# Three edits to the Mamba layer of a four-layer kernel: taps of two conv blocks in turn, tokens that arrive turned, three small products as transposes

## The chip, the cores and the metric

The kernel runs on one core of one Trainium2 chip. Time is device microseconds (us) of one execution. The kernel before took 1125.33, 1127.39 and 1128.77 us in three runs (median 1127.39). The engines are named as in the profile: PE (TensorE, matmuls), PEld (its weight loads), DVE (VectorE), ACT (ScalarE), POOL (GpSimd), SP (SyncE, which here only issues DMAs). Each runs its own instructions in program order, and waits on semaphores for the others.

## The reference

Four layers, each followed by a residual sum and a layer norm, on 2048 tokens of 512 features in float32. All of the change lies in the first, a Mamba-2 mixer over two sequences of 1024 tokens:

```python
zxbcdt = einsum('bld,di->bli', x, W_in)          # gate 1024, xBC 1024+16+16, dt 16
conv = conv_b
for k in range(4):
    conv = conv + xpad[:, k:k + l, :] * conv_w[:, k]
xBC = silu(conv)                                  # -> x (16 heads of 64), B, C
dt = softplus(dt + dt_bias);  dA = exp(dt * -exp(A_log))
h = h * dA + (dt * x) B ;  y = h C                # scan over the tokens
y = (y + D_skip * x) * silu(gate)
y = y * rsqrt(mean(y * y) + eps) * norm_w
x = layernorm(x + einsum('bld,do->blo', y, W_out))
```

The three layers behind it (a ternary product bounded by tanh, an RG-LRU block, a gated FFN on int32 codes) are the same in both kernels.

## The kernel before, in words

Features lie on the 128 partitions, tokens along the free dimension. Every float32 product is made of three fp32r products: each operand is split into a high part (`..h`, a rounded copy made by ACT) and a low part (`..l`, the difference, made by DVE), and `three` in the PE's program multiplies high by high, high by low and low by high.

`mamba2` works in 8 steps s = 0 to 7, alternately of the one sequence and of the other. A step is 256 tokens, two chunks j of 128. No scheduler orders anything: each engine has a function (`sync`, `gpsimd`, `scalar`, `vector`, `tensor`) with a loop over s that is written out by hand, and work of step s+1 is started in the second half of step s. The parts that the prediction speaks of are these.

- Turning the tokens. SP loads the tokens of a step into `a_xf`, tokens on partitions. `turn` on PE (line 809) transposes them in 8 blocks into the banks `ps_t`, `turn` on ACT (393) copies them rounded into `a_xth`, `turn` on DVE (583) makes `a_xtl`. PE does it for s+1 right behind the last gate product of step s, DVE between `cumulate(s)` and the second `scan`.
- Projections. `x_proj` (8 blocks m, in pairs p) and `gate` (the same) are 96 matmuls of 256 columns each per step; `out_proj` 24 of 512 columns per chunk. All have line 801, that of `three`.
- The convolution. ACT's `evict` (443, 446) copies a pair of blocks to `a_xpre` and writes the fourth tap with the bias into `a_xs`. On DVE `conv_m` adds the other three taps to one block by `taps` (575): each tap reads and writes the same tile as the tap before it, and `order` makes DVE wait for its end. There are 8 blocks a step, so 24 taps and 16 such waits. Between them stand `low` (701) and the pieces of the norm: `mean_sq` (615), `residual` (623, 625, 627), `normalize` (633). `residual` needs `a_rs`, which POOL's `scale` (338) makes from what `mean_sq` wrote.
- The decays. ACT's `decay` and `bc_out` (414 to 419) give the decays and C; `turn_a` (829) before them and `gram` (836, 838) behind them are small PE products; `turn_z` (822) is another. ACT's `gram` (424, 426) copies the result to `a_btok` and `a_gs`, and the PE's `out_proj` of the second chunk may start only when `a_gs` has been read out of its bank.
- The scans. DVE's `scan` (658) runs four scans of 512 elements per chunk over `a_L`, `cumulate` (646) four of 128 over `a_ex`, each with a wait for the one before it though they write different parts.
- The end of a step. DVE updates the state (680), adds the outputs from the banks (688), gates them (695), and makes the decays of the next step (`soft`, 596 to 610). ACT's `high_y` (434) and `square` (438) need the gated values, and `decay` comes behind them in ACT's order. POOL's `tree` (331 to 333) sums the squares.

Of the kernel before, what the change touches and what calls it, by code (L numbers as in the profile page):

```python
# [59 lines left out]
class Order:  # L60
# [5 lines left out]
    def __call__(self, ins):  # L66
        self.count += 1
        ins.then_inc(self.sem, 1)
        self.eng.wait_ge(self.sem, self.count)
# [14 lines left out]
def mamba2(nc, signals, psum, ident, powers, x_in, x_out, da_d, c_d, w_x, w_bc, w_gate, w_out, conv, a_log, dt_bias, d_skip, norm_w, fill, space, following):  # L84
# [35 lines left out]
    xf = sb("a_xf", [P, C, D], F32)  # L120
# [55 lines left out]
    s_xt, s_xh, s_xl = sem("xt"), sem("xh"), sem("xl")  # L176
# [43 lines left out]

    def sync(sp, following_stage):
        def load_x(s):
            for j in range(C):
                wait(sp, s_xt, C * (s - 1) + j + 1)
                sp.dma_start(xf[:, j, :], chunk(x_in, s, j)).then_inc(s_x[j], 16)
# [44 lines left out]
        for s in range(NS):  # L270
# [8 lines left out]
            else:  # L279
                if s == NS - 1:  # L280
                    sp.wait_ge(s_xt, C * NS)
# [96 lines left out]
    def scalar(act, following_stage):  # L378
# [180 lines left out]
    def vector(dve, following_stage):  # L559
        order = Order(dve, s_dve)  # L560

# [73 lines left out]
        def conv_m(s, m):  # L635
            i = M * s + m
            dve.wait_ge(s_acc, i + 1)
            dve.wait_ge(s_pre, 4 * s + m // 2 + 1)
# [13 lines left out]
        def scan(n):  # L652
# [142 lines left out]
    def tensor(pe, following_stage):  # L795
# [1247 lines left out]
```

## Time and profile before

| | before |
|---|---|
| three runs, us | 1125.33, 1127.39, 1128.77 |
| span of the profiled execution, us | 1127.5 |
| PE, PEld busy, us | 1076.4, 939.6 |
| DVE, ACT, POOL busy, us | 749.1, 572.9, 318.6 |
| granted TensorE clock, mean | 0.980 |
| the Mamba layer, us from the start | 0 to about 445 |

The profiled execution is given by its span, from the first to the last instruction; it is 0.1 us from the median of the runs. "Busy" is the time in which at least one instruction of an engine was running; for PE the ends are modelled, and its share of busy time overstates how full it is. DVE is 96% busy in the steps of the Mamba layer and 31% in the last layer, so shares are read by stage.

### The profile page before, as it was taken

Reading aid. Unit: us, or ns where it says so; the run is one execution under the profiler, and the core shown is the slowest. Engines: PE = TensorE matmul, PEld = TensorE weight load, DVE = VectorE, ACT = ScalarE, POOL = GpSimd, SP = SyncE. Lnnn points to the kernel's source line nnn. Section 1 sums busy time; section 2 is a strip of 40 time slices with the busy share of each in tenths; the row PEclk is TensorE's granted clock in tenths of the full one; section 3 lists DMA queues with packets and bytes.
Section 4 is the critical chain, followed back from the end, with each engine's and each line's share of the span. In section 5 each row is a group of like instructions: output and inputs, shape, how many; then the busy total and the mean of one; then the engine's idle time right before and its main releaser. Section 6 shows DMA issues by size and latency. Waiting matters only on the chain.

```text
span 1127.5 us, 18155 instructions
## 1 busy us (share of the span) xinstructions
PE 1076.4 (95%) x6912; PEld 939.6 (83%) x6912; DVE 749.1 (66%) x1311; ACT 572.9 (51%) x1190; POOL 318.6 (28%) x433
## 2 busy tenths in 40 slices
PE   6899999999999997899999999899999999999997
PEld 6788888888888886788998998887888888888886
DVE  6899999999999988857766687765342233223213
ACT  6857666667757674565666556653312311321320
POOL 1012222130403123333444434414312311321331
PEclk9889999999999998999999999999999999999999
DMA  5504031312213055411011101408012002002001
GB/s 198 200 3 147 12 137 45 103 52 95 91 57 126 3 201 198 143 55 38 1 38 39 39 1 39 141 19 299 0 38 75 1 19 94 1 1 75 1 1 56
DMA packets 41590, 81.22 MB, mean 72 GB/s; under 512 B 7456, under 2 KB 13472, under 8 KB 39456
## 3 DMA queue, kind: packets, MB, share of 16 engines
q1 hardware_dynamic: 41504, 80.06, 21.2%
q8 instruction: 55, 0.90, 0.3%
q14 instruction: 31, 0.25, 0.1%
HBM read 67.19 MB, written 12.85 MB: 71 GB/s over the span
## 4 chain that ended last, share of the span: by engine, by line
PE 57%; DVE 26%; ACT 7%; issue 6%; POOL 3%; DMA 2%; DVEq 0%; SPq 0%; POOLq 0%; ACTq 0%
PE banks L1870 20%; PE banks L1883 11%; PE banks L801 9%; PE banks L1518 8%; DVE a_L L658 5%; DVE a_xs L575 4%; PE banks L1486 4%; PE banks L931 2%; DVE a_ygl L701 1%; DVE a_L L672 1%; DVE c_gx L1377 1%; PE banks L923 1%; DMA c_xb<-tokens 1%; ACT c_a L1252 1%; DVE a_stats L625 1%
## 5 line engine op out<-in xcount | busy, mean ns | idle before, releaser
L1770 ACT ACTIVATE d_sg<-banks,d_gs 128x512 f32<-128x512 f32 x64 | 44.0, 688 | 224.9 <-PE banks L1870 224.9
L1813 DVE SCALAR_TENSOR_TENSOR d_h<-banks,d_us,d_sg 128x512 f32<-128x512 f32 x64 | 48.1, 751 | 163.7 <-PE banks L1870 151.3
L1744 POOL TENSOR_TENSOR d_hl<-d_h,d_hh 128x512 fp32r<-128x512 f32 x64 | 83.2, 1300 | 158.3 <-ACT d_hh L1774 158.2
L575 DVE SCALAR_TENSOR_TENSOR a_xs<-a_xpre,a_cvec,a_xs 128x256 f32<-128x256 f32 x192 | 100.3, 537 | 7.1 <-ACT a_xs L446 2.5
L1883 PE MATMUL banks<-d_wd,d_hh 128*128 128x512 f32 x256 | 101.1, 395 | 0.0
L1883 PE MATMUL banks<-d_wd,d_hl 128*128 128x512 f32 x256 | 100.9, 394 | 0.0
L331 POOL TENSOR_TENSOR a_sg<-a_sg 128x512 f32<-128x512 f32 x16 | 24.6, 1535 | 220.1 <-ACT a_sg L438 220.1
L658 DVE TENSOR_TENSOR_SCAN a_L<-a_L,a_ident 128x512 f32<-128x512 f32 x64 | 78.4, 1225 | 2.2
L801 PE MATMUL banks<-a_xth,a_wxh 128*128 128x256 f32 x256 | 76.7, 299 | 0.0
L462 ACT ACTIVATE a_xdt<-banks,a_dt 128x64 f32<-128x64 f32 x256 | 56.3, 349 | 37.1 <-PE banks L881 37.1
L801 PE MATMUL banks<-a_xth,a_wgh 128*128 128x256 f32 x256 | 75.0, 293 | 0.0
L801 PE MATMUL banks<-a_xtl,a_wxh 128*128 128x256 f32 x256 | 74.1, 289 | 0.0
L801 PE MATMUL banks<-a_xth,a_wxl 128*128 128x256 f32 x256 | 74.0, 289 | 0.0
L801 PE MATMUL banks<-a_xth,a_wgl 128*128 128x256 f32 x256 | 72.9, 285 | 0.0
L801 PE MATMUL banks<-a_xtl,a_wgh 128*128 128x256 f32 x256 | 72.8, 284 | 0.0
L801 PE MATMUL banks<-a_woh,a_ygh 128*128 128x512 f32 x128 | 55.0, 429 | 5.6 <-ACT a_gs L426 3.7
L1883 PEld LDWEIGHTS banks<-d_wd,d_hl 128*128 128x128 f32 x256 | 48.1, 188 | 11.2
L1883 PEld LDWEIGHTS banks<-d_wd,d_hh 128*128 128x128 f32 x256 | 48.2, 188 | 11.0
L801 PEld LDWEIGHTS banks<-a_xth,a_wxh 128*128 128x128 f32 x256 | 50.5, 197 | 4.7 <-issue 4.1
L801 PE MATMUL banks<-a_woh,a_ygl 128*128 128x512 f32 x128 | 52.7, 412 | 0.0
L801 PE MATMUL banks<-a_wol,a_ygh 128*128 128x512 f32 x128 | 52.6, 411 | 0.0
L1870 PE MATMUL banks<-d_xtl,d_wg_late 128*128 128x512 f32 x128 | 51.5, 402 | 0.0
(285 smaller groups left out, 3151.9 us busy)
## 6 DMA issues: line engine op xcount, KB each, us to landing
a_L<-decays SPq DMA_DIRECT2D x16, 1024.0 KB, 5.2
a_xf<-in_x SPq DMA_DIRECT2D x16, 256.0 KB, 3.1
a_xr<-in_x SPq DMA_DIRECT2D x16, 256.0 KB, 2.8
tokens<-a_xr SPq DMA_DIRECT2D x16, 256.0 KB, 4.0
c_xb<-tokens SPq DMA_DIRECT2D x16, 256.0 KB, 3.2
d_xin<-tokens SPq DMA_DIRECT2D x16, 256.0 KB, 4.8
d_r<-tokens SPq DMA_DIRECT2D x16, 256.0 KB, 2.7
d_wd_codes<-in_down_w SPq DMA_DIRECT2D x4, 1024.0 KB, 9.4
```

Source lines behind the costliest of these rows:

```text
L331: order(pool.tensor_tensor(sq[:, 0:4], sq[:, 0:4], sq[:, 4:8], ALU.add))
L462: ins = act.activation(xdt[:, j, h * HD:(h + 1) * HD], ps_t[:, q % 2, 2 * j + i // 2, i % 2 * HD:(i % 2 + 1) * HD], ACT.Copy, scale=dt[:, ...
L575: ins = dve.scalar_tensor_tensor(out=dst, in0=src[:, k:k + T], scalar=vec[:, k:k + 1], in1=dst, op0=ALU.mult, op1=ALU.add)
L658: order(dve.tensor_tensor_scan(own, own, ident4.rearrange("p h t -> p (h t)"), 0.0, ALU.mult, ALU.add))
L801: last = pe.matmul(out, lhs(i, k), rhs(c, k), start=(k, i, c) == (0, 0, 0), stop=(k, i) == (n - 1, 1))
L1486: done = pe.matmul(ps_x, x[:, k, cols(j)], wp[:, k, :], start=i == 0, stop=i == 3 * KD - 1)
L1518: done = pe.matmul(ps_x[:, q, m % 2, :], wp[:, k, m * P:(m + 1) * P], x[:, k, :], start=i == 0, stop=i == 3 * KD - 1)
L1744: pool.tensor_tensor(hl[:, m, :], h32[:, m % 2, :], hh[:, m, :].bitcast(F32), ALU.subtract).then_inc(s_hl, 1)
L1770: act.activation(sg[:, m % 2, :], ps_g[:, m % 2, :], ACT.Silu, scale=gs[:, m:m + 1]).then_inc(s_sg, 1)
L1813: dve.scalar_tensor_tensor(out=h32[:, m % 2, :], in0=ps_u[:, m % 2, :], scalar=us[:, m:m + 1], in1=sg[:, m % 2, :], op0=ALU.mult, op1=ALU. ...
L1870: ins = pe.matmul(out[:, m % 2, :], w(k, m), x[:, k, :], start=(k == 0 and x is xth), stop=(k == KD - 1 and x is xtl))
L1883: ins = pe.matmul(ps_o[:, c % 2, :], h[:, m, cols(c)], wd[:, m, :], start=(m == 0 and h is hh), stop=(m == M - 1 and h is hl))
```

## The change

On DVE the taps of two blocks alternate: tap 0 of block 2p, tap 0 of block 2p+1, tap 1 of block 2p, and so on, where each tap from the second on waits for the tap before it on its own block. `Order` gets two halves for that: `mark` counts an instruction, `after` waits for a count. The scans of `scan` and `cumulate` are marked and no longer waited for one by one; the first instruction that reads their result waits for the last. `low` and the two `mean_sq` move to the places between pairs.

The host hands the tokens over a second time, turned (`x_turned`), features on partitions. `a_xf` has the same size and is loaded from there; ACT and DVE make `a_xth` and `a_xtl` from it, and PE's `turn` is gone with its waits. ACT's `turn` now waits until the gate products that read `a_xth` are done, SP's next load waits for DVE's `turn` and no longer for PE's.

Three small PE products with the identity (`turn_z`, `turn_a`, the first half of `gram`) are written as transposes.

```diff
     def __call__(self, ins):
+        self.after(self.mark(ins))
+
+    def mark(self, ins):
         self.count += 1
         ins.then_inc(self.sem, 1)
-        self.eng.wait_ge(self.sem, self.count)
+        return self.count
+
+    def after(self, count):
+        self.eng.wait_ge(self.sem, count)
...
             for j in range(C):
-                wait(sp, s_xt, C * (s - 1) + j + 1)
-                sp.dma_start(xf[:, j, :], chunk(x_in, s, j)).then_inc(s_x[j], 16)
+                wait(sp, s_xl, C * (s - 1) + j + 1)
+                sp.dma_start(xf[:, ks(j), :], x_turned[s % B * NT + s // B, :, ks(j), :]).then_inc(s_x[j], 16)
...
         def turn(s):
+            wait(act, s_gate, 4 * s)
             for j in range(C):
-                act.wait_ge(s_xt, C * s + j + 1)
-                act.activation(xth[:, :, cols(j)], ps_t[:, j], ACT.Copy).then_inc(s_xh, 1)
+                act.wait_ge(s_x[j], 16 * s + 16)
+                act.activation(xth[:, ks(j), :], xf[:, ks(j), :], ACT.Copy).then_inc(s_xh, 1)
...
-                dve.tensor_tensor(xtl[:, :, cols(j)], ps_t[:, j], xth[:, :, cols(j)].bitcast(F32), ALU.subtract).then_inc(s_xl, 1)
+                dve.tensor_tensor(xtl[:, ks(j), :], xf[:, ks(j), :], xth[:, ks(j), :].bitcast(F32), ALU.subtract).then_inc(s_xl, 1)
...
+        def conv_pair(s, p):
+            pair = (2 * p, 2 * p + 1)
+            tapped = {}
+            dve.wait_ge(s_pre, 4 * s + p + 1)
             wait(dve, s_halo, s)
-            taps(xs[s % 2][:, m, :], xpre[:, m, :], cvec[:, m, :], s_xc)
+            for k in range(3):
+                for m in pair:
+                    out = xs[s % 2][:, m, :]
+                    if k == 0:
+                        dve.wait_ge(s_acc, M * s + m + 1)
+                    else:
+                        order.after(tapped[m])
+                    ins = dve.scalar_tensor_tensor(out=out, in0=xpre[:, m, k:k + T], scalar=cvec[:, m, k:k + 1], in1=out,
+                                                   op0=ALU.mult, op1=ALU.add)
+                    if k < 2:
+                        tapped[m] = order.mark(ins)
+                    else:
+                        ins.then_inc(s_xc, 1)
...
                 for j in range(C):
-                    order(dve.tensor_tensor_scan(ex[:, g, cols(j)], ex[:, g, cols(j)], zero.broadcast_to([P, P]), 1.0, ALU.mult, ALU.add))
+                    last = order.mark(dve.tensor_tensor_scan(ex[:, g, cols(j)], ex[:, g, cols(j)], zero.broadcast_to([P, P]), 1.0, ALU.mult, ALU.add))
             wait(dve, s_su, G * C * s)
+            order.after(last)
...
-                order(dve.tensor_tensor_scan(own, own, ident4.rearrange("p h t -> p (h t)"), 0.0, ALU.mult, ALU.add))
+                scanned[j] = order.mark(dve.tensor_tensor_scan(own, own, ident4.rearrange("p h t -> p (h t)"), 0.0, ALU.mult, ALU.add))
...
             wait(dve, s_stp, n - C + 1)
+            order.after(scanned[j])
...
-            conv_m(s, 4)
+            conv_pair(s, 2)
             if s:
                 mean_sq(C * s - 2)
-            conv_m(s, 5)
-            if s:
                 mean_sq(C * s - 1)
                 residual(C * s - 2)
-            conv_m(s, 6)
-            conv_m(s, 7)
+            conv_pair(s, 3)
...
-        def turn(s):
-            for j in range(C):
-                pe.wait_ge(s_x[j], 16 * s + 16)
-                wait(pe, s_xdt, 4 * (s - 1) + 2 + j + 1)
-                for k in range(KD):
-                    last = pe.transpose(ps_t[:, j, k, :], xf[:, j, k * P:(k + 1) * P], ident)
-                last.then_inc(s_xt, 1)
...
-                last = pe.matmul(ps_f[0:H, cols(j)], a[:, j, :], ident, start=True, stop=True)
+                last = pe.transpose(ps_f[0:H, cols(j)], a[:, j, :], ident)
...
             pe.wait_ge(s_xs, 4 * s + q + 1)
-            if q < 2:
-                pe.wait_ge(s_xl, C * s + q + 1)
-            else:
-                pe.wait_ge(s_xdt, 4 * s + q - 2 + 1)
+            wait(pe, s_xdt, 4 * s + q - 2 + 1)
...
     dram("x", x.reshape(-1, P, D))
+    dram("x_turned", x.reshape(-1, 2 * P, KD, P).transpose(0, 3, 2, 1))
```

On DVE, from the last gating of a step to the first `residual` of the next; in brackets stands what a row waits for (`a_dve_order` is DVE's own earlier work). Before:

```order
L695 TENSOR_TENSOR a_xs_81<-a_xs_81,a_sg 128x8x128 [waits a_sg,a_ya]
L575 SCALAR_TENSOR_TENSOR a_xs_99<-a_xpre,a_cvec,a_xs_99 128x256 [waits a_halo,a_pre,a_acc]
L575 SCALAR_TENSOR_TENSOR a_xs_99<-a_xpre,a_cvec,a_xs_99 128x256 [waits a_dve_order] x2
L701 TENSOR_TENSOR a_ygl_93<-a_xs_81,a_ygh_91 128x1024 [waits a_yh]
...
L615 TENSOR_SCALAR a_rs<-banks 128x1 [waits a_ssqp]
L575 SCALAR_TENSOR_TENSOR a_xs_99<-a_xpre,a_cvec,a_xs_99 128x256 [waits a_halo,a_pre,a_acc]
L575 SCALAR_TENSOR_TENSOR a_xs_99<-a_xpre,a_cvec,a_xs_99 128x256 [waits a_dve_order] x2
L615 TENSOR_SCALAR a_rs<-banks 128x1 [waits a_ssqp]
L623 SCALAR_TENSOR_TENSOR a_xr<-banks,a_rs,a_xr 128x512 [waits a_rs,a_xr0,a_op]
```

And now, in the changed kernel's line numbers (658 the taps, 726 `low`, 626 `mean_sq`, 634 `residual`):

```order
L720 TENSOR_TENSOR a_xs_81<-a_xs_81,a_sg 128x8x128 [waits a_sg,a_ya]
L658 SCALAR_TENSOR_TENSOR a_xs_99<-a_xpre,a_cvec,a_xs_99 128x256 [waits a_acc,a_halo,a_pre]
L658 SCALAR_TENSOR_TENSOR a_xs_99<-a_xpre,a_cvec,a_xs_99 128x256 [waits a_acc]
L658 SCALAR_TENSOR_TENSOR a_xs_99<-a_xpre,a_cvec,a_xs_99 128x256 [waits a_dve_order] x4
L726 TENSOR_TENSOR a_ygl_93<-a_xs_81,a_ygh_91 128x1024 [waits a_yh]
...
L626 TENSOR_SCALAR a_rs<-banks 128x1 [waits a_ssqp] x2
L634 SCALAR_TENSOR_TENSOR a_xr<-banks,a_rs,a_xr 128x512 [waits a_rs,a_xr0,a_op]
```

`low` has moved behind three more taps, the first `mean_sq` has gone back behind the taps of block 5, and the three taps that stood between it and `residual` no longer do.

On PE, from the end of `gate(s, 3)` to the next step's first product (909, now 918, is `state`; 923 and 931, now 932 and 940, are `scan_out`). Before:

```order
L801 MATMUL banks<-a_xth,a_wgl 128x256
L809 MATMUL banks<-ident,a_xf 128x128 x8
L909 MATMUL banks<-a_xdt,a_bw 64x256 x4
L923 MATMUL banks<-a_ex,a_S 128x128 x8
L931 MATMUL banks<-a_L_82,a_xdt 64x128 x16
```

And now:

```order
L821 MATMUL banks<-a_xth,a_wgl 128x256
L918 MATMUL banks<-a_xdt,a_bw 64x256 x4
L932 MATMUL banks<-a_ex,a_S 128x128 x8
L940 MATMUL banks<-a_L_82,a_xdt 64x128 x16
```

The 8 transposes of the tokens are gone; nothing else has changed places on PE.

## Rows read from the trace of the kernel before

**Rows 1.** The page: the span, and the busy time of each engine.
```profile
span 1127.5 us, 18155 instructions
PE 1076.4 (95%) x6912; PEld 939.6 (83%) x6912; DVE 749.1 (66%) x1311; ACT 572.9 (51%) x1190; POOL 318.6 (28%) x433
```

**Rows 2.** Busy time by stretch; columns as in the first line.
```profile
core 0: us, PE busy (x) PEld busy (x) DVE busy (x) ACT busy (x) POOL busy (x), PEclk, DMA share, GB/s
186.57:237.93 51.36, 49.84 (x409) 44.38 (x408) 49.22 (x87) 35.32 (x88) 12.12 (x17) 1.00 0.25 81
```

**Rows 3.** Waits of DVE in 83.7 to 340 us: total, times, longest.
```profile
DVE a_xs L688 <- PE banks L931: 0.9, 5, 0.2
```

**Rows 4.** DVE in order of time: start, us, line, tiles, times; around step 3.
```profile
183.91 1.52 DVE L575 SCALAR_TENSOR_TENSOR a_xs<-a_xpre,a_cvec,a_xs 128x256 f32<-128x256 f32 x3
193.71 0.15 DVE L615 TENSOR_SCALAR a_rs<-banks 128x1 f32<-128x1 f32 x1
212.94 1.28 DVE L583 TENSOR_TENSOR a_xtl<-banks,a_xth 128x512 fp32r<-128x512 f32 x2
214.30 5.00 DVE L658 TENSOR_TENSOR_SCAN a_L<-a_L,a_ident 128x512 f32<-128x512 f32 x4
223.88 0.87 DVE L680 SCALAR_TENSOR_TENSOR a_S<-a_S,a_et,a_tmp 128x256 f32<-128x256 f32 x2
235.27 1.53 DVE L575 SCALAR_TENSOR_TENSOR a_xs<-a_xpre,a_cvec,a_xs 128x256 f32<-128x256 f32 x3
```

**Rows 5.** ACT in order of time, step 3.
```profile
189.49 0.42 ACT L419 ACTIVATE a_cs<-a_bcs 16x256 f32<-16x256 f32 x1
211.01 0.60 ACT L475 ACTIVATE a_sg<-banks 128x512 f32<-128x512 f32 x1 [0.94 <-PE banks L801]
211.51 1.08 ACT L393 ACTIVATE a_xth<-banks 128x512 fp32r<-128x512 f32 x2
```

**Rows 6.** PE in order of time, step 3.
```profile
191.04 0.60 PE L860 MATMUL banks<-a_ones,a_sg 128*128 128x1 f32 x4
192.06 0.47 PE L801 MATMUL banks<-a_woh,a_ygh 128*128 128x512 f32 x1 [0.41 <-ACT a_gs L426]
210.69 0.28 PE L801 MATMUL banks<-a_xth,a_wgl 128*128 128x256 f32 x1
210.81 1.03 PE L809 MATMUL banks<-ident,a_xf 128*128 128x128 f32 x8
235.03 0.61 PE L829 MATMUL banks<-ident,a_a 128*16 128x128 f32 x4
```

**Rows 7.** POOL in order of time, step 3.
```profile
193.94 0.72 POOL L338 TENSOR_TENSOR a_rs<-a_rs,powers 128x1 f32<-128x1 f32 x1 [4.75 <-DVE a_rs L615]
```

**Rows 8.** Groups: line, tiles, shapes, times, busy us, mean ns.
```profile
L658 DVE TENSOR_TENSOR_SCAN a_L<-a_L,a_ident 128x512 f32<-128x512 f32 x64 | 78.4, 1225 | 2.2
L1377 DVE TENSOR_TENSOR_SCAN c_gx<-c_a,c_hlast,c_gx 128x256 f32<-128x256 f32 x32 | 21.4, 733 | 0.3
L452 ACT ACTIVATE a_xs<-a_xs 128x512 f32<-128x512 f32 x32 | 20.4, 665 | 0.0
L393 ACT ACTIVATE a_xth<-banks 128x512 fp32r<-128x512 f32 x16 | 8.6, 596 | 0.0
```

**Rows 9.** DVE in order of time, the RG-LRU layer and step 6.
```profile
506.39 2.68 DVE L1377 TENSOR_TENSOR_SCAN c_gx<-c_a,c_hlast,c_gx 128x256 f32<-128x256 f32 x4
338.14 1.52 DVE L575 SCALAR_TENSOR_TENSOR a_xs<-a_xpre,a_cvec,a_xs 128x256 f32<-128x256 f32 x3
367.92 1.29 DVE L583 TENSOR_TENSOR a_xtl<-banks,a_xth 128x512 fp32r<-128x512 f32 x2 [0.65 <-ACT a_xth L393]
```

**Rows 10.** Busy time behind the small products of steps 5 and 6.
```profile
294.90:298.30 3.40, 3.37 (x17) 2.84 (x18) 3.26 (x10) 0.93 (x2) 0.86 (x2) 1.00 0.80 309
347.60:351.00 3.40, 3.40 (x11) 2.62 (x10) 3.28 (x8) 0.00 (x0) 1.27 (x2) 0.50 0.42 138
```

**Rows 11.** The chain that ended last, at `turn_z(1)`: start, us, what.
```profile
61.49 1.03 PE banks L822 x4
```

More of the change, by code:

```diff
@@ L81, in inverse_root, with mamba2 @@
     return pool.tensor_tensor(out, v, powers[:, 1:2].broadcast_to(v.shape), ALU.pow)
-def mamba2(nc, signals, psum, ident, powers, x_in, x_out, da_d, c_d, w_x, w_bc, w_gate, w_out, conv, a_log, dt_bias, d_skip, norm_w, fill, space, following):
+def mamba2(nc, signals, psum, ident, powers, x_in, x_turned, x_out, da_d, c_d, w_x, w_bc, w_gate, w_out, conv, a_log, dt_bias, d_skip, norm_w, fill, space, following):
     T = 256
@@ L119, in mamba2 @@
     at_xf = sb.at
-    xf = sb("a_xf", [P, C, D], F32)
+    xf = sb("a_xf", [P, KD, T], F32)
     xpre = sb("a_xpre", [P, M, HALO + T], F32)
@@ L175, in mamba2 @@
     s_x, s_xr, s_st = ([sem(f"{n}{j}") for j in range(C)] for n in ("x", "xr", "st"))
-    s_xt, s_xh, s_xl = sem("xt"), sem("xh"), sem("xl")
+    s_xh, s_xl = sem("xh"), sem("xl")
     s_bp, s_bcr, s_bacc, s_bconv, s_bhalo, s_cs = (sem(n) for n in ("bp", "bcr", "bacc", "bconv", "bhalo", "cs"))
@@ L219, in rows, with ks @@
         return slice(r * 64, (r + 1) * 64)
+    def ks(j):
+        return slice(j * KD // C, (j + 1) * KD // C)
     def sync(sp, following_stage):
@@ L280, in sync @@
                 if s == NS - 1:
-                    sp.wait_ge(s_xt, C * NS)
+                    sp.wait_ge(s_xl, C * NS)
                     following_stage["load_x"](0)
@@ L560, in vector @@
         order = Order(dve, s_dve)
+        scanned = {}
         def low_piece(i):
@@ L633, in normalize @@
             dve.tensor_scalar(out, out, mv[:, j, 0:1], mv[:, j, 2:3], ALU.subtract, ALU.mult).then_inc(s_done, 1)
[L635 to L638, printed above, removed]
+        def conv_pair(s, p):
+            pair = (2 * p, 2 * p + 1)
+            tapped = {}
+            dve.wait_ge(s_pre, 4 * s + p + 1)
             wait(dve, s_halo, s)
-            taps(xs[s % 2][:, m, :], xpre[:, m, :], cvec[:, m, :], s_xc)
+            for k in range(3):
[11 more added lines that the diff above has]
+                        ins.then_inc(s_xc, 1)
         def cumulate(s):
@@ L716, in vector @@
         for s in range(NS):
-            conv_m(s, 0)
+            conv_pair(s, 0)
             if s:
                 low(C * s - 1)
-            conv_m(s, 1)
-            if s == 0:
+            else:
                 low_piece(NX)
                 low_piece(NX + 1)
-            conv_m(s, 2)
-            conv_m(s, 3)
+            conv_pair(s, 1)
             if s == 0:
@@ L821, in turn_z @@
             for j in range(C):
-                last = pe.matmul(ps_f[:, 256 + j * H:256 + (j + 1) * H], bcr[Z0:Z0 + H, HALO + j * P:HALO + (j + 1) * P],
-                                 ident[Z0:Z0 + H, Z0:Z0 + H], start=True, stop=True)
+                last = pe.transpose(ps_f[:, 256 + j * H:256 + (j + 1) * H], bcr[Z0:Z0 + H, HALO + j * P:HALO + (j + 1) * P],
+                                    ident[Z0:Z0 + H, Z0:Z0 + H])
             last.then_inc(s_zt, 1)
@@ L835, in gram @@
             for j in range(C):
-                pe.matmul(ps_f[:, j * N:(j + 1) * N], bcs[0:N, cols(j)], ident[0:N, 0:N], start=True, stop=True)
+                pe.transpose(ps_f[:, j * N:(j + 1) * N], bcs[0:N, cols(j)], ident[0:N, 0:N])
             for j in range(C):
@@ L933, in scan_out @@
                 last.then_inc(s_yp, 1)
-        pe.wait_ge(s_const, 2)
-        turn(0)
         pe.wait_ge(s_const, 15 + HQ)
@@ L966, in tensor @@
             gate(s, 3)
-            if s + 1 < NS:
-                turn(s + 1)
-            else:
+            if s + 1 == NS:
                 following_stage["turn_in"](0)
@@ L1938, in build @@
             split.append((raw, d[name].rearrange("(k p) n -> p k n", p=P), *W[n]))
-        first, last, parts, ends = mamba2(nc, signals, psum, ident, powers, x, between[0], decays, readouts, d["w_x"], d["w_bc"], d["w_gate"],
+        first, last, parts, ends = mamba2(nc, signals, psum, ident, powers, x, d["x_turned"], between[0], decays, readouts, d["w_x"], d["w_bc"], d["w_gate"],
                                           d["w_out0"], d["conv0"], d["A_log"], d["dt_bias"], d["D_skip"], d["norm_w"], fill_identity,
```

## The prediction

> **What bounds the kernel now.** I read the busy shares first. PE is busy 95% of the span and DVE 66% [rows 1], which would leave DVE out of it. By stage it looks otherwise: in a whole step of the Mamba layer DVE is busy 49.22 of 51.36 us, and PE 49.84, whose ends are modelled [rows 2]. So the waits come next. Over the five steps from 83.7 to 340 us DVE waits for another engine for 0.9 us in all, always at the same place, the last outputs from the banks [rows 3]. DVE thus sets the pace of these steps: each of its instructions starts when the one before it allows.
>
> I call E the start of the first tap of a step. E is 183.91 us in step 3 and 235.27 in step 4 [rows 4], so a step takes 51.36 us. DVE being full does not say what a faster DVE is worth. For that I follow the other way round the loop, from E through ACT and PE back to DVE. Gating ends at E; then ACT runs `high_y`, `square`, the decays and C without a gap, and `a_cs` is done at 189.91 (E + 6.0) [rows 5]. PE makes its small products, waits for ACT's copy `a_gs`, and starts `out_proj` of the second chunk at 192.06 (E + 8.15) [rows 6]. From there PE has no wait until the last gate matmul of 210.69 ends at 210.97. ACT's silu starts at 211.01, `a_xth` at 211.51 [rows 5, 6], and DVE's `turn` comes at 212.94, E + 29.03 [rows 4]. The two `a_xth` take 596 ns each [rows 8], so the first is there at 211.51 + 0.60 = 212.11. DVE comes only 0.8 us later than it could. That slack of 0.8 us in the first half of a step, against a DVE gain larger than it, is the heart of this forecast.
>
> **The change part by part, per full step.**
>
> Taps. Three taps on one block take 1.52 us from the start of the first to the end of the last [rows 4]; two pairs of start to start of 0.52 and one run of 0.48. Where two instructions of 256 elements don't depend on each other, `a_S`, both together take 0.87 us at 0.48 each [rows 4], so the second starts 0.39 after the first. The cost of a dependence is thus 0.52 - 0.40 = 0.12 us, and 16 of the 24 taps have one: 1.92 us. Alternating, a tap is called 0.8 us after the tap that it needs, which ends after 0.48. I take 0.12; the ends are 0 and 0.13 each, from the same rows.
>
> Scans. Four scans in a row take 5.00 us, the last of them 1.225 [rows 4, 8], so they start (5.00 - 1.225) / 3 = 1.26 apart: 0.035 goes to each wait. A scan without a wait stands in the RG-LRU layer: four take 2.68 us at 0.733 each [rows 8, 9], 0.65 apart, against the 0.77 that 0.733 and 0.035 would give. Saving 0.12 each: 4 x 0.12 = 0.48 per chunk, once in each half of the step. The four small scans of `cumulate` give 3 x 0.12 = 0.36, in the first half. Bounds 0 and 0.15 each.
>
> Residual. The two `mean_sq` now stand together right ahead of `residual`, which needs POOL's power of the first. POOL starts 0.23 us after `mean_sq` and takes 0.72 [rows 4, 7] (193.71, 193.94 to 194.66). Before, three taps lay over it; now DVE waits from 0.14 to about 1.00 us: +0.86. Behind `residual` in DVE's queue stand the last six taps, the scans and `turn`. Bounds 0.5 and 1.2, the power's 0.72 us taken half as long and half as long again.
>
> DVE reaches `turn` at 29.03 - 1.92 - 0.48 - 0.36 + 0.86 = E + 27.13. It can't start before `a_xth`, at 212.11 + 0.04 = 212.15, E + 28.24. ACT and PE take what they took on that way, since none of their work on it is touched but two small products: `gram` loses two instructions of 0.11 us, yet `a_gs` follows ACT's own queue, which stands before it. So `turn` comes at 28.24 instead of 29.03: 0.8 us earlier, not 1.9. The new residual wait is hidden in the 1.1 us that DVE would wait anyway. POOL's `tree` lies beside the first taps as before.
>
> `a_xth` and `a_xtl` now read the SBUF instead of a bank. ACT takes 665 ns for 512 elements from there in `a_xs` and 596 from a bank [rows 8]: between -0.05 and +0.07 us; I take 0.
>
> From `turn` to the next E is 235.27 - 212.94 = 22.33 us [rows 4]. Of it goes 0.48 by the scans of the second chunk. PE has lost its 8 transposes, 1.03 us [rows 6], just ahead of `state`; it comes 1.0 us earlier there, and so keeps ahead of a DVE that is 0.8 earlier. `turn_a` and `turn_z` lose two instructions each, 0.61 us for four [rows 6], so 0.2 to 0.3 us; neither ends a wait of DVE. They cost nothing and give nothing here. The second half becomes 21.85.
>
> A step: 28.24 + 21.85 = 50.09, down 1.27 us. Steps 1 to 5: -6.4.
>
> SP. The next load of `a_xf` waits for DVE's `turn`, some 2 us later than for PE's. Behind it in SP's queue is the transfer of the decays, 25 us away. Nothing.
>
> Step 0 and the start. The first `x_proj` waits for the weights, not for the tokens. `turn_z(1)` lies on the chain that ended last, at half clock, 1.03 us for four [rows 11]: -0.4.
>
> Steps 6 and 7. Here `turn` waited for `a_xth` already: it comes at 367.92, 29.78 behind E at 338.14, with 0.65 us of waiting [rows 9]. Only the second half gains: -0.5 each, -1.0.
>
> **The clock.** In step 6, behind the small products and the wait for `a_gs`, PE ran at 0.50 of its clock, 1.2 instead of 2.4 GHz, from 347.6 to 351.0; at the same place of step 5 at 1.00 [rows 10]. Step 7 has the same fall. It cost PE 29.78 - 28.24 = 1.5 us, of which DVE's slack took half. Now no slack is left, and each such fall costs the whole 1.5. And they may come more often: PE reaches the small products 0.2 us earlier and has two fewer of them, so it idles longer in front of `a_gs`, where it idled 0.41 us in step 3 [rows 6]. How many of steps 1 to 5 fall I can't read; the trace has none of five there and two of two in steps 6 and 7. I take two: +3.0. The ends are none and all five (+7.5).
>
> In the Trainium skill, "TensorE: Matmul & The Clock Gate", Part 4: PE-mode transpose, says that work in transpose mode does not count as PE being busy in the same way. Here 8 transposes of the tokens ran in 1.03 us with the clock at 1.00 in that whole step [rows 2, 6]; whether the three small ones matter no row tells. By the rule more steps would fall, up to the end of all five, 1127.2 by the sum below.
>
> **Sum.** 1127.5 (the span, 0.1 from the median) - 6.4 - 0.4 - 1.0 + 3.0 = 1122.7. I say 1122.5. What comes after 445 us is unchanged and starts earlier by the same amount.
>
> **Rivals.**
>
> The clock falls in every step: 1127.5 - 7.8 + 7.5 = 1127.2. For it: no slack, more idling. Against: five of seven steps were free of it.
>
> The clock falls no more than before: 1119.7.
>
> DVE gets all that it saves, because ACT and PE come earlier too: 51.36 - 1.92 - 0.96 - 0.36 + 0.86 = 48.98 a step, 2.4 less, times seven 16.7: 1110.8. Against it stand the 18.9 us of PE work without a gap from `a_gs` to the last gate matmul [rows 6], which nothing shortens.
>
> Slower: the waits cost nothing, so taking them away gives nothing, while the residual wait stands. Then `turn` is at 29.03 + 0.86 and the second half at 22.33: 0.86 more a step, times seven 6.0, less 0.4: 1133.1. It decides once taps and scans of the first half save less than 0.86 of the 2.76 us counted. That is what the Trainium skill would give: "VectorE: DVE Perf Modes", The DRAIN you can't avoid, says that the next operation starts only when the pipeline is empty, that eight copies took the same with a semaphore after each as with one at the end, and that semaphores need not be saved. Against it: the pair `a_S` overlaps by 0.09 us and the four scans by 0.08 each [rows 4, 9], at full length in each row. This row is of this kernel, and I follow it.
>
> **Numbers.** One to three more falls of the clock, 1121 to 1124.5: 0.43. None more: 0.25. Four or five: 0.17. All of DVE's gain: 0.06. Slower by the residual wait: 0.09. No change means within 0.3%, 3.4 us, of 1127.4, about what can be told apart here: 1124.0 to 1130.8. Faster then holds 0.25, 0.06 and most of the first, 0.35: 0.66. The same: the rest of the first, 0.16 of the clock in every step and 0.02 of the last: 0.26. Slower: 0.08. The range leaves out the fourth case and most of the last: 1114 to 1129.
>
> **What would show it.** In the changed profile: taps of a pair in 2.4 us (0.40 apart) instead of 2.9; four scans in 4.6 to 4.7; a wait of DVE for POOL ahead of `residual` of 0.8 to 0.9 us; a new wait of DVE's `turn` for ACT's `a_xth` near 1.1 us; E + 28.2 for `turn`; steps of 50.1 us at full clock and of 51.6 with a fall. I am wrong if `turn` doesn't wait (then DVE's own sum decides), if taps stand 0.52 apart, or if full-clock steps are not 1.0 to 1.5 us shorter.

## The result, and the profile after

| | before | after |
|---|---|---|
| median, us (15 executions each) | 1128.5 (1125.33 to 1130.57) | 1123.06 (1121.81 to 1126.62) |
| ratio, 95% interval | | 0.9961 (0.9952 to 0.997) |
| span of the profiled execution, us | 1127.5 | 1123.2 |
| mean granted clock in it | 0.980 | 0.975 |

The changed kernel is 0.39% faster: 5.4 us between the medians, where 4.9 against the first median of 1127.4 had been forecast. The page shows where instructions went: PE has 112 fewer, DVE as many as before but 15.8 us less busy [rows 1].

```profile
span 1123.2 us, 17876 instructions
PE 1061.2 (94%) x6800; PEld 927.2 (83%) x6800; DVE 733.3 (65%) x1311; ACT 573.0 (51%) x1190; POOL 321.8 (29%) x433
```

The steps come next. By stretch, the changed kernel: step 1 (whole at full clock), step 3 (with a fall of the clock), then the falls of steps 2 to 5 and 7, and the same place of step 6, which has none (columns as in [rows 2]).

```profile
80.98:130.85 49.87, 47.92 (x396) 42.93 (x396) 47.01 (x88) 35.14 (x87) 12.85 (x16) 1.00 0.26 84
182.62:233.94 51.32, 49.40 (x396) 44.02 (x395) 47.10 (x87) 35.13 (x87) 12.85 (x16) 0.97 0.25 81
139.31:142.72 3.41, 3.41 (x10) 2.63 (x9) 2.68 (x9) 0.46 (x1) 1.07 (x2) 0.50 0.72 271
190.51:193.92 3.41, 3.28 (x8) 2.63 (x9) 2.71 (x9) 1.02 (x2) 1.06 (x2) 0.50 0.80 305
241.71:245.12 3.41, 3.15 (x8) 2.51 (x9) 2.71 (x9) 1.15 (x3) 0.97 (x2) 0.50 0.78 305
292.91:296.32 3.41, 2.88 (x7) 2.33 (x8) 2.72 (x10) 1.42 (x5) 0.70 (x2) 0.50 0.87 321
395.31:398.72 3.41, 3.41 (x10) 2.66 (x9) 2.68 (x7) 0.01 (x1) 1.07 (x2) 0.50 0.62 210
344.10:347.50 3.40, 2.88 (x13) 2.35 (x14) 2.70 (x10) 1.42 (x5) 0.69 (x2) 1.00 0.90 323
```

The steps without a fall take 49.87 us (step 1) and 49.80 (step 6), against 51.36 of [rows 2]. Those with one take 51.2 to 51.8. So five falls stand at this place in steps 1 to 7 where the trace before had two. (Falls from 33 us behind the last E on, where the layer ends, stand in every kernel's trace and are not counted.) From E of step 1 to E of step 7 it is 305.4 us, after 309.3: 3.9 less, where six steps of 49.85 would give 10.2 less.

DVE's side of step 1 (start, duration, both us; a wait and its releaser in brackets):

```profile
80.98 2.46 DVE L658 SCALAR_TENSOR_TENSOR a_xs<-a_xpre,a_cvec,a_xs 128x256 f32<-128x256 f32 x6
91.88 0.75 DVE L634 SCALAR_TENSOR_TENSOR a_xr<-banks,a_rs,a_xr 128x512 f32<-128x512 f32 x1 [0.70 <-POOL a_rs L347]
109.10 1.30 DVE L594 TENSOR_TENSOR a_xtl<-a_xf,a_xth 128x512 fp32r<-128x512 f32 x2 [0.90 <-ACT a_xth L403]
110.46 4.57 DVE L682 TENSOR_TENSOR_SCAN a_L<-a_L,a_ident 128x512 f32<-128x512 f32 x4
```

Six taps take 2.46 us, where two blocks took 2.9 [rows 4]; four scans 4.57 where they took 5.00. `turn` comes at E + 28.12, after 0.90 us of waiting for `a_xth`. DVE's waits in 80 to 340 us (total, times, longest) answer to [rows 3], which had one row:

```profile
DVE a_xtl L594 <- ACT a_xth L403: 8.7, 5, 2.0
DVE a_xr L634 <- POOL a_rs L347: 3.5, 5, 0.7
DVE a_xr L634 <- PE banks L821: 1.2, 4, 0.4
DVE a_xs L713 <- PE banks L940: 0.9, 5, 0.2
```

DVE now waits 14.3 us in five steps. The first row is the cap of the first half: 0.9 in the step at full clock and 2.0 in the four with a fall. PE and ACT at the small products of step 1:

```profile
86.36 0.28 PE L821 MATMUL banks<-a_xth,a_wxl 128*128 128x256 f32 x1
87.02 0.29 PE L848 MATMUL banks<-ident,a_bcs 16*128 16x16 f32 x2 [0.39 <-ACT a_cs L429]
87.17 0.69 PE L850 MATMUL banks<-a_cs,a_bcs 16*128 16x128 f32 x4
87.79 0.61 PE L872 MATMUL banks<-a_ones,a_sg 128*128 128x1 f32 x4
89.00 0.47 PE L821 MATMUL banks<-a_woh,a_ygh 128*128 128x512 f32 x1 [0.61 <-ACT a_gs L436]
```
```profile
86.88 0.57 ACT L453 ACTIVATE a_xpre<-banks 128x512 f32<-128x512 f32 x1
87.47 1.02 ACT L456 ACTIVATE a_xs<-banks,a_cvec 128x256 f32<-128x256 f32 x2
88.47 0.39 ACT L436 ACTIVATE a_gs<-banks 128x256 f32<-128x256 f32 x1
```

PE waits twice here, 0.39 for `a_cs` and 0.61 for `a_gs` (before: 0.41 for `a_gs` in the step of [rows 6], 0.56 to 0.57 in most others, and under 0.1 ahead of it), and starts `out_proj` of the second chunk at E + 8.02. ACT evicts the last pair of blocks (453, 456) between `a_cs` and `a_gs`: PE's products are there before ACT is free to copy them.

### The profile page after: what moved, and what is told of

Its sections match the earlier page's. It is cut to its first block, busy times and chain, and to the rows that moved or that the text cites. A ratio compares the mean times of both kernels' runs of the same rounds, so it can differ in the third digit from the quotient of the medians.

```text
span 1123.2 us, 17876 instructions
## 1 busy us (share of the span) xinstructions
PE 1061.2 (94%) x6800; PEld 927.2 (83%) x6800; DVE 733.3 (65%) x1311; ACT 573.0 (51%) x1190; POOL 321.8 (29%) x433
## 4 chain that ended last, share of the span: by engine, by line
PE 61%; DVE 18%; ACT 10%; issue 5%; POOL 3%; DMA 2%; SPq 1%; POOLq 0%; DVEq 0%; ACTq 0%
PE banks L1875 21%; PE banks L821 13%; PE banks L1888 11%; PE banks L1523 8%; PE banks L1491 4%; DVE a_L L682 2%; PE banks L940 2%; DVE c_gx L1382 1%; PE banks L890 1%; PE banks L932 1%; DVE a_ygl L726 1%; ACT L428 1%; ACT L424 1%; DVE c_cv L1358 1%; ACT a_xs L456 1%
## 5 line engine op out<-in xcount | busy, mean ns | idle before, releaser
L340 POOL TENSOR_TENSOR a_sg<-a_sg 128x512 f32<-128x512 f32 x16 | 31.1, 1943 | 223.7 <-ACT a_sg L448 223.7
L658 DVE SCALAR_TENSOR_TENSOR a_xs<-a_xpre,a_cvec,a_xs 128x256 f32<-128x256 f32 x192 | 90.1, 538 | 2.8 <-ACT a_xs L456 2.8
L682 DVE TENSOR_TENSOR_SCAN a_L<-a_L,a_ident 128x512 f32<-128x512 f32 x64 | 73.1, 1205 | 0.5
L821 PEld LDWEIGHTS banks<-a_xth,a_wxh 128*128 128x128 f32 x256 | 50.4, 197 | 5.1 <-issue 3.9
L1875 PE MATMUL banks<-d_xtl,d_wg_late 128*128 128x512 f32 x128 | 51.5, 402 | 0.0
```

What stands on the lines that cost most here:

```text
L340: order(pool.tensor_tensor(sq[:, 0:4], sq[:, 0:4], sq[:, 4:8], ALU.add))
L658: ins = dve.scalar_tensor_tensor(out=out, in0=xpre[:, m, k:k + T], scalar=cvec[:, m, k:k + 1], in1=out, op0=ALU.mult, op1=ALU.add)
L682: scanned[j] = order.mark(dve.tensor_tensor_scan(own, own, ident4.rearrange("p h t -> p (h t)"), 0.0, ALU.mult, ALU.add))
L821: last = pe.matmul(out, lhs(i, k), rhs(c, k), start=(k, i, c) == (0, 0, 0), stop=(k, i) == (n - 1, 1))
L1875: ins = pe.matmul(out[:, m % 2, :], w(k, m), x[:, k, :], start=(k == 0 and x is xth), stop=(k == KD - 1 and x is xtl))
```

## The experiments

Times are medians beside the kernel before on the same chip. The step is one at full clock in the profiled execution, E to E; "turn" is DVE's `turn` behind E, "rest" from there to the next E.

| kernel | us | ratio to before (95%) | step | turn | rest | mean clock of its timed executions |
|---|---|---|---|---|---|---|
| before | 1128.1 to 1129.4 | 1 | 51.36 | 29.03 | 22.33 | 0.983 (68) |
| changed | 1123.06 | 0.9961 (0.9952 to 0.997) | 49.87 | 28.12 | 21.75 | 0.978 (15) |
| scans_only | 1124.41 | 0.9955 (0.994 to 0.9969) | 50.78 | 28.32 | 22.46 | 0.984 (9) |
| taps_only | 1127.0 | 0.9977 (0.9964 to 0.999) | 50.83 | 28.37 | 22.46 | 0.983 (12) |
| turned_only | 1129.31 | 1.0005 (0.9991 to 1.002) | 51.37 | 29.04 | 22.33 | 0.982 (12) |
| small_undone | 1124.36 | 0.9972 (0.9959 to 0.9984) | 50.25 | 28.33 | 21.92 | 0.979 (11) |
| filler | 1117.27 | 0.9908 (0.9895 to 0.992) | 49.97 | 28.05 | 21.92 | 0.985 (4) |
| before_filler | 1127.02 | 0.9991 (0.998 to 1.0002) | 51.33 | 29.02 | 22.31 | 0.985 (11) |
| filler_mean | 1117.36 | 0.9905 (0.9889 to 0.9921) | 49.85 | 28.09 | 21.75 | 0.985 (5) |
| filler_turns | 1119.64 | 0.9919 (0.9903 to 0.9935) | 50.23 | 28.09 | 22.14 | 0.984 (6) |
| filler_serial | 1123.02 | 0.995 (0.9934 to 0.9965) | 50.99 | 29.07 | 21.92 | 0.983 (6) |
| gram_first | 1121.28 | 0.9942 (0.9928 to 0.9956) | 49.40 | 27.63 | 21.77 | 0.978 (6) |
| gram_filler | 1114.86 | 0.9883 (0.9868 to 0.9898) | 49.33 | 27.57 | 21.77 | 0.983 (4) |
| chain_short | 1111.81 | 0.986 (0.9845 to 0.9875) | 49.09 | 27.31 | 21.78 | 0.985 (4) |

### One part alone, put into the kernel before

scans_only is this, and the same in `cumulate`:

```diff
-                order(dve.tensor_tensor_scan(own, own, ident4.rearrange("p h t -> p (h t)"), 0.0, ALU.mult, ALU.add))
+                scanned[j] = order.mark(dve.tensor_tensor_scan(own, own, ident4.rearrange("p h t -> p (h t)"), 0.0, ALU.mult, ALU.add))
...
+            order.after(scanned[j])
```

> The kernel before with only the scans of scan and cumulate unmarked (one wait behind the last in place of one behind each). Theory 1, the loop from E over ACT and PE caps the first half at E + 28.1 to 28.2: DVE would reach turn at 29.03 - 0.48 - 0.36 = E + 28.19, which just meets that cap, and the second half becomes 22.33 - 0.48 = 21.85; steps at full clock of 50.0 to 50.1 us, steps with a fall of the clock of 51.4, so nearly all of the whole change's gain: 1123 to 1124.5 us, ratio 0.996. Rival, the parts add up in proportion to what they take off DVE (1.32 of 2.4 us net a step): 1125.5, ratio 0.9975. Rival, a wait between scans costs nothing: 1128.5.

taps_only takes `conv_pair` and the new places of `low` and `mean_sq`:

> The kernel before with only the taps in pairs and low and mean_sq in their new places; scans waited for one by one, tokens turned on PE. Theory 1: DVE would reach turn at 29.03 - 1.92 + 0.7 = E + 27.8, the cap makes it 28.2, the second half stays 22.3: 50.5 a step at full clock, 51.9 with a fall. With four falls in seven steps that is 2.3 us less than before: 1126, ratio 0.998; with none 5.6 less. Rival, the parts in proportion (1.06 of 2.4): 1126 as well, but then with steps of 50.1 at full clock and no wait of turn. Rival, slower by the wait for POOL: 1133.

turned_only takes `x_turned` and loses PE's `turn`:

> The kernel before with only the tokens handed over turned: 64 transposes less on PE, 1.03 us a step just ahead of state. Theory 1: PE's second half waits for nobody, and DVE for nobody in it: no difference, 1128 to 1129, ratio 0.9995 to 1.0005, steps of 51.4. Rival, PE bounds the second half: up to 1.0 a step, 1121.5.

Turned tokens alone give nothing, as both steps and the time say. taps_only has about the time that was expected, but steps of 50.8 and not 50.5: turn comes 0.2 us later and its second half is no shorter than before. The scans alone give as much time as the whole change, which rules out that parts count in proportion. The cap stood where it was put, turn at 28.3 to 28.4 in both kernels. But the second half of scans_only stayed at 22.46, although four scans in it are 0.43 shorter. Its waits of DVE, 83 to 340 us:

```profile
DVE a_xtl L590 <- ACT a_xth L399: 3.2, 2, 1.7
DVE a_z L595 <- PE banks L831: 2.6, 5, 0.5
```

The second row is new: 0.5 us in each step for `turn_z`. With PE's own transposes of the tokens left in, PE bounds the second half. So the steps are 50.8 and not 50.0; the time was still as forecast, because this execution had two falls in steps 1 to 7, and the clock over its timed executions is 0.984 against the changed kernel's 0.978. The whole change has steps 0.9 us shorter than scans_only and hands it back in falls.

### The clock

filler puts work that nobody reads into PE's two waits:

```diff
+        def filler(s, count):
+            wait(pe, s_xdt, 4 * s)
+            for k in range(count):
+                pe.matmul(ps_t[:, 0].rearrange("p k t -> p (k t)"), wo[0][:, k, 0:P], wo[0][:, k, :], start=True, stop=True)
...
             x_proj(s, 3)
+            if s:
+                filler(s, 2)
             gram(s)
...
             if s:
+                filler(s, 2)
                 out_proj(C * s - 1, 0)
```

> The changed kernel with four more PE products a step (512 columns, operands always there, result never read): two in the wait ahead of gram, two in the wait for a_gs. They compute nothing that is needed. Theory, the falls of the clock come from PE's idling at that place and cost up to 1.6 us each: no fall at that place in steps 1 to 7, steps of 49.9 to 50.0 us each, so six steps take 299.5 in place of 305.4 in the changed kernel's profile: 1117.5, ratio to before 0.990, mean granted clock 0.984 or more. Rival, the falls do not depend on how long PE idles there: as the changed kernel, 1123 to 1124, ratio 0.996. Rival, the added products are on the path (0.22 each): 1123 + 5 = 1128.

Measured: 1117.27 us, no fall in steps 1 to 7, all of them 49.8 to 50.4. PE at the place that follows step 4's E (231.52), and a whole step:

```profile
236.85 0.62 PE L871 MATMUL banks<-a_woh 128*128 128x512 f32 x2
237.56 0.30 PE L848 MATMUL banks<-ident,a_bcs 16*128 16x16 f32 x2
238.79 0.71 PE L871 MATMUL banks<-a_woh 128*128 128x512 f32 x2
239.54 0.47 PE L821 MATMUL banks<-a_woh,a_ygh 128*128 128x512 f32 x1
```
```profile
231.52:281.48 49.96, 48.92 (x400) 43.36 (x399) 47.17 (x87) 35.10 (x87) 12.78 (x16) 1.00 0.25 83
```

`out_proj` starts at E + 8.02, as without the filler: four more products cost nothing, and 5.8 us are gone. That products put into PE's idle time at this place take the falls away, and that every step then takes about 50, is shown. Then the same in the kernel before:

> The kernel before with the same four added products a step (they compute nothing that is needed), two ahead of gram and two ahead of out_proj of the second chunk. Theory: without falls in steps 1 to 7 all its steps take 51.4; a fall costs the kernel before only 0.9, DVE's slack taking the rest, and it has some two to four of them: 1126, ratio 0.998. Against filler's 1117.3 the change is then worth 9 us, where it was worth 5.4 with falls. Rival, a fall costs both kernels the same: the kernel before gains 6 as well, 1122.5, ratio 0.995.

Measured 1127.02, steps of 51.33 to 51.34: 1.3 us gained, inside the interval, near the theory and far from the rival's 6. Between the two fillers lie 9.75 us (1127.02 - 1117.27, on two chips whose kernels before differ by 0.1). That is what the change is worth when PE keeps its clock; 4.3 of it were lost to falls. There are more of them, and each costs 1.3 to 1.9 us where it cost 0.9 before (step 6, 52.23 against 51.36), DVE's slack hiding the rest.

small_undone has the three products as before:

> The changed kernel with the three small products as matmuls with the identity again. Theory: out_proj of the second chunk starts 0.28 later (E + 8.3, as in the runs of single parts), turn at 28.35 in place of 28.12, steps at full clock of 50.1; the idling is as long as in the changed kernel, so falls are as frequent: 1124 to 1125, ratio 0.9965. Rival, products in transpose mode do not count as work for the clock, so that as matmuls they prevent the falls: clock 0.984, 1118 to 1119, ratio 0.991.

Turn came at 28.2 to 28.4 in its three steps without a fall, and the clock is as low as the changed kernel's (0.979 and 0.978). Written as matmuls the products do not keep the clock. But one premise of the theory is not in the trace: PE does not idle here as long as in the changed kernel. Waits of PE in 83 to 340 us, the changed kernel first, then small_undone:

```profile
PE banks L821 <- ACT a_gs L436: 3.0, 5, 0.6
PE banks L848 <- ACT a_cs L429: 2.2, 5, 0.5
PE banks L821 <- ACT a_gs L436: 2.4, 5, 0.6
```

Added up from the timelines, gap by gap, PE's idle time between the last product of `x_proj` and `out_proj` of the second chunk is this, in steps 1 to 7, beside the mean clock of the timed executions:

| kernel | idle, us a step | mean clock |
|---|---|---|
| before, scans_only, taps_only, turned_only | 0.48 to 0.57 | 0.982 to 0.984 |
| small_undone | 0.47 to 0.57 | 0.979 |
| gram_first (below) | 0.5 to 0.7 | 0.978 |
| changed | 1.0 to 1.15 | 0.978 |
| filler, gram_filler (below) | 0 to 0.12 | 0.985, 0.983 |

Filling the idle time ends the falls. But its length does not tell how many there are: small_undone idles no longer than the kernel before and has the changed kernel's clock. Why the changed kernel falls more often stays open.

### The prediction's own steps, with the clock held

filler_mean, where `conv_pair` calls what it is given behind its first two taps:

```diff
-            conv_pair(s, 2)
+            conv_pair(s, 2, lambda: mean_sq(C * s - 2) if s else None)
             if s:
-                mean_sq(C * s - 2)
```

> filler with mean_sq of the first chunk put back between the taps of the third pair, so that residual need not wait for POOL (0.7 us a step). Theory, the wait is hidden behind turn's wait for a_xth, which becomes 1.5 in place of 0.9: steps of 50.0 as in filler, 1117.3, ratio 0.991. Rival, DVE sets the pace: 0.7 us less in each of seven steps, 1112.5, ratio 0.9865.

1117.36 against 1117.27. DVE's first wait, in 83 to 340 us, is now this, and the row on `a_rs` is gone; filler had 4.2 and 3.5:

```profile
DVE a_xtl L594 <- ACT a_xth L403: 8.3, 5, 1.7
```

The wait for POOL was moved into the wait for `a_xth`, nothing else. It was hidden, as forecast.

filler_turns has the tokens turned on PE:

> filler with the tokens turned on PE again (8 transposes a step ahead of state); taps, scans and small products as in the changed kernel, the four added products kept. Theory, which scans_only suggests: with DVE faster the second half waits for PE, at turn_z, unless the transposes are gone: turn at E + 28.1, second half 22.45 in place of 21.8 to 21.9, steps of 50.5, 3.5 to 4.5 us more than filler: 1121, ratio 0.994. Rival, the prediction's own step (PE keeps ahead with or without them): as filler, 1117.3, ratio 0.991.

1119.64, 2.4 us more than filler by the medians and 1.2 by the ratios, whose intervals overlap. The steps are clearer: 0.26 longer, 1.8 us over seven, with a wait for `turn_z` of 0.2 in each:

```profile
DVE a_z L595 <- PE banks L838: 1.0, 5, 0.2
```

That lies between the two: less than the theory's price, but not nothing. The rival is not quite the prediction's own step, which was that PE keeps ahead because it comes 1.0 us earlier without the transposes. Where the other 0.3 of scans_only's wait went was not run apart; filler_turns has `turn_z` as a transpose, scans_only as a matmul.

filler_serial runs the taps of a block in a row (`for m in pair: for k in range(3)`):

> filler with the three taps of a block in a row again, each waiting for the one before it; low and mean_sq stay between the pairs. Theory: DVE reaches turn 1.92 later than by itself now, at 27.2 + 1.9 = E + 29.1, later than a_xth allows (28.1): steps of 50.9 in place of 49.97, so half of what alternating saves counts and half is waiting: 6.5 us more than filler, 1124, ratio 0.9965. Rival, all of the taps' saving lies in turn's wait: 1117.3. Rival, all of it counts: 1130.

1123.02, turn at 29.07 without a wait. About half of what alternating saves (1.0 of 1.9 a step) counts.

### Shorter caps

gram_first:

```diff
             bc_out(s)
-            evict(s, 3)
             gram(s)
+            evict(s, 3)
```

> The changed kernel with one line of ACT's program moved: gram(s), which copies a_gs out of its bank, ahead of evict(s, 3). Theory, the way from E over ACT and PE caps the first half: PE's small products end at about E + 6.8, a_gs starts at about E + 6.9 in place of 7.49, out_proj of the second chunk at 7.4 to 7.5 in place of 8.02, turn at 27.5 in place of 28.12 (DVE by itself would be there at 27.2): steps at full clock of 49.3 in place of 49.85. PE also idles about half a microsecond less there, so fewer falls. With no fall 1114 to 1115, with as many as now 1119; I take 1116, ratio 0.989. Rival, DVE sets the pace or the eviction now late holds up the last pair of taps or the gate products: no gain, 1123.

ACT now waits for PE, and PE for nobody behind the small products (rows of ACT and PE, step 4, E at 231.15):

```profile
238.06 0.20 ACT L434 ACTIVATE a_btok<-banks 128x32 f32<-128x32 f32 x1 [0.93 <-PE banks L850]
238.16 0.38 ACT L436 ACTIVATE a_gs<-banks 128x256 f32<-128x256 f32 x1
```
```profile
237.96 0.61 PE L872 MATMUL banks<-a_ones,a_sg 128*128 128x1 f32 x4
238.68 0.47 PE L821 MATMUL banks<-a_woh,a_ygh 128*128 128x512 f32 x1
```

`a_gs` at E + 7.0, `out_proj` at 7.5, turn at 27.6, steps of 49.4: as worked out. The time, 1121.28, is not the 1116 I took, but the one for many falls: the profiled execution had one in steps 1 to 7 (1119.30 us), the others a clock down to 0.974. PE idles 0.5 to 0.7 us a step here, not much longer than the kernels with a clock of 0.983, and the shorter idling was not enough.

gram_filler adds two of the filler's products ahead of `gram`:

> gram_first with two added products a step ahead of gram (computing nothing that is needed), none behind the small products, where PE has no wait left. Theory: gram_first's full-clock steps of 49.4 to 49.5 in all of steps 1 to 7, against filler's 49.97: 3.5 to 4 us less than filler, 1113.5, ratio 0.987. Rival, two products are too few to keep the clock: 1116 to 1119.

1114.86, no fall in steps 1 to 7, steps of 49.3 to 49.7: the rival's 1116 to 1119 is out, the theory's 1113.5 missed by 1.4. chain_short changes several things at once, as its expectation lists. On ACT the second `square` moves too:

```diff
                 high_y(C * s - 1)
-                square(C * s - 1)
             decay(s)
             bc_out(s)
+            if s:
+                square(C * s - 1)
             gram(s)
```

> gram_first, and the second square of the step moved behind bc_out on ACT, so that a_cs ends about 1.04 earlier, at E + 4.95, and PE's gram follows x_proj at E + 5.5 without a wait; sum_sq of the second chunk behind the first x_turn, mean_sq of both chunks between taps; two added products ahead of out_proj of the second chunk. Theory: a_gs at about E + 6.4, out_proj at 6.9 in place of 7.4, xth allows turn at 27.0; DVE by itself is there at 26.5 to 27.2, depending on whether POOL, whose tree now starts 3 us later, still makes residual wait. Steps of 48.8 to 49.0 in place of 49.45: 1110 to 1111, ratio 0.9845. Rival, POOL's later tree holds up the norm and with it DVE: no better than gram_filler, 1113.5, or worse.

1111.81: the fastest, 1.4% under the kernel before and 1.0% under the changed one (0.986 over 0.9961), with two products a step that nobody needs. `out_proj` starts at E + 7.1 and not 6.9, turn comes at 27.15 to 27.3 and not at 27.0. DVE's waits (83 to 340 us):

```profile
DVE a_xr L645 <- POOL a_mv L87: 2.7, 6, 0.4
DVE a_xs L716 <- PE banks L946: 0.9, 5, 0.2
DVE a_xtl L595 <- ACT a_xth L403: 0.5, 3, 0.2
```

`turn` waits 0.5 us in five steps: ACT and PE hardly cap the first half any more; DVE and its waits for POOL do.

## Why the prediction held, step by step

**What bounds.** That the way from E over ACT and PE caps what a faster DVE can give was right, and it carries the result. The cap was forecast at E + 28.24 and is 28.12; full-clock steps were to be 50.09 and are 49.80 to 49.87.

**Taps and scans.** Taps: 2.4 us a pair forecast, 2.46 measured. Scans: 4.6 to 4.7 forecast, 4.57 measured. The rival that ended slower rested on waits that cost nothing. Here a wait costs 0.12 us between two taps and (5.00 - 4.57) / 3 = 0.14 between two scans. The Trainium skill's page "VectorE: DVE Perf Modes", The DRAIN you can't avoid, says that a semaphore behind each of eight copies cost nothing extra; for these taps and scans the runs show the opposite. The same section says that a next operation that is not held starts earlier, which agrees with the 0.12 and 0.14.

**The wait for POOL.** 0.8 to 0.9 forecast, 0.70 measured, hidden (filler_mean). **The new wait of `turn`.** 1.1 forecast, 0.90 measured.

**The step that failed** is the one on PE's small products, "They cost nothing and give nothing here", with the reason that `a_gs` follows ACT's own queue. In the first half the products as transposes bring turn from 28.3 to 28.1 (small_undone against the changed kernel). `a_gs` follows PE as well: with them as matmuls it starts at E + 7.76 (turned_only) and not at 7.49. The way leads over ACT's eviction of the last pair, which stands ahead of `a_gs` and waits for `x_proj`; `x_proj` in its turn comes behind `turn_a`, the first small product (small_undone, step 4, E at 232.85):

```profile
232.56 0.61 PE L841 MATMUL banks<-ident,a_a 128*16 128x128 f32 x4
239.01 0.60 ACT L453 ACTIVATE a_xpre<-banks 128x512 f32<-128x512 f32 x1 [0.16 <-PE banks L821]
```

So the eviction starts at E + 6.16, and at E + 5.90 in the changed kernel, where `turn_a` takes 0.38. The three products were not run apart; the rows point to `turn_a`.

In the second half the prediction was right: DVE keeps what its scans save because PE comes earlier without the token transposes; in scans_only, which has them, PE makes DVE wait 0.5 a step. `turn_z` as a transpose gave nothing here: small_undone has it as a matmul, and its second half is 21.92 without a wait for it. The gain of a step was 1.5 and not 1.27.

**The clock.** The term was mis-sized. Two more falls in steps 1 to 5 were taken, +3.0 us; the profile has four there. They cost as forecast: steps with one are 1.3 to 1.9 us longer than those without. In steps 6 and 7 one of two fell away. Against a mean clock of 0.983 before stands 0.978 over the timed executions, so the falls are no accident of the profiled one.

That the total came within 0.6 us of 1122.5 is luck in part. From E of step 1 to E of step 7 the forecast gives 6.4 + 0.5 - 3.0 = 3.9 us less, and 3.9 were measured, but out of other terms. The falls of steps 2 to 5 took 6.3 us, 3.3 more than was put down. Against that, steps 1 to 5 without their falls gained 1.4 more than forecast, and step 6, which was to be 0.5 shorter, is 2.4 shorter (52.23 to 49.80), its fall being gone.

Longer idling was one reason offered for more falls. Filling the idle time takes them away, but the idle times and clocks of small_undone and gram_first speak against its length as the cause. Another was the mode of the small products. By the Trainium skill, "TensorE: Matmul & The Clock Gate", Part 4: PE-mode transpose, work in transpose mode does not count as PE being busy in the same way. small_undone has the three products as matmuls and the same low clock, so no run here shows that the mode of these products matters.

**Why several in a row.** At this place a fall starts 7.5 to 9.8 us behind E in every trace. In the changed kernel those of steps 2 to 5 start 8.5, 7.9, 7.8 and 7.5 us behind E (139.31 - 130.85, and so on), and a step with a fall takes 51.2 to 51.8: the next fall meets its step at almost the same point. A step without one is 1.5 shorter, like step 6. In scans_only, taps_only and turned_only a step with a fall takes 52.2 to 52.5, and no more than two follow one another; in small_undone it takes 51.5 to 51.7, and two follow one another once; gram_first has one alone. That one fall calls for the next, and that the shorter steps have more falls for this reason, is my reading; no run shows it apart.

## What to carry to other kernels

A gain on the engine that waits for nobody is worth no more than the slack of the way round through the others: follow that loop before summing, and look at each half of a step by itself, since the edit that "gives nothing" alone can be the one that lets another count (turned tokens: 0 alone, 0.26 us a step once taps and scans are faster). When a stage gets shorter, look at TensorE's clock again: here the change was worth 9.75 us with the clock held and 5.4 without care for it, and four products a step in TensorE's idle time gave 5.8 us. And compare the durations of like instructions, not only the waits: a loss of 1.6 us a step on DVE, told below, stands in no row of waits.

## What the runs showed of the hardware that I had not expected

POOL's tree and DVE hold each other up. In the kernel before, the tree's first sum over 512 elements started at 186.12, when DVE's `low` (1.22 us, two SBUF inputs) was 0.77 under way, and took 1.60. In the changed kernel the two start together, and the taps around them are these:

```profile
184.20 0.88 DVE L658 SCALAR_TENSOR_TENSOR a_xs<-a_xpre,a_cvec,a_xs 128x256 f32<-128x256 f32 x2
184.82 2.54 POOL L340 TENSOR_TENSOR a_sg<-a_sg 128x512 f32<-128x512 f32 x1 [3.76 <-ACT a_sg L448]
184.99 1.22 DVE L726 TENSOR_TENSOR a_ygl<-a_xs,a_ygh 128x1024 fp32r<-128x1024 f32 x1
186.13 1.51 DVE L658 SCALAR_TENSOR_TENSOR a_xs<-a_xpre,a_cvec,a_xs 128x256 f32<-128x256 f32 x1
```

The sum takes 2.54, 0.94 more, and `low` nothing more. But three taps behind `low` take 1.51, 0.96 and 0.67 us where the others take 0.48. The kernel before has the same: 1.52, 0.84 and 0.56 at E + 2.6, 4.1 and 5.0. Added up, DVE loses 1.55 to 1.65 us in each of steps 1, 3 and 4 of both kernels, as much as the change gains in one. chain_short shows that it is the tree: there it starts at E + 6.2 and not at 2.2, and the long taps (1.36, 0.96, 0.69) stand at E + 6.8, 8.1 and 9.0 and not at 3.5, 5.0 and 5.8. The change neither makes nor cures this loss, so it does not enter the forecast; what a tree out of DVE's way would be worth was not run, and in the changed kernel the cap on `turn` would hide it.

filler_serial has the other order (step 3, E at 183.00):

```profile
185.21 1.39 POOL L340 TENSOR_TENSOR a_sg<-a_sg 128x512 f32<-128x512 f32 x1 [3.98 <-ACT a_sg L448]
185.48 1.40 DVE L658 SCALAR_TENSOR_TENSOR a_xs<-a_xpre,a_cvec,a_xs 128x256 f32<-128x256 f32 x1
186.67 0.80 POOL L341 TENSOR_TENSOR a_sg<-a_sg 128x256 f32<-128x256 f32 x1
186.80 1.75 DVE L726 TENSOR_TENSOR a_ygl<-a_xs,a_ygh 128x1024 fp32r<-128x1024 f32 x1
187.55 1.32 POOL L342 TENSOR_TENSOR a_sg<-a_sg 128x128 f32<-128x128 f32 x1
```

Here POOL starts first and keeps its time, 1.39 and 0.80, and DVE's tap and `low` take 0.92 and 0.53 longer; POOL's last sum, which starts behind `low`, takes 1.32 where it takes 0.52 in the changed kernel. The Trainium skill, "SBUF — State Buffer", Who interferes with whom, says that a VectorE instruction with two SBUF inputs contends with a GpSimd instruction that reads SBUF, and that the order of issue decides who is blocked. These rows agree. In the changed kernel POOL's sum is recorded 0.17 us ahead of `low`, but a tap was running when it started (to 185.08), so it does not speak against the order.
